# Attention scores of two heads on the two row halves of TensorE, with a fourth bank for max scores and a new order within each pair

## What is computed

```python
q, k, v = split(x @ qkv_w.T + qkv_b)                 # 16 heads of 16
scores  = where(causal, q @ k.T * 16**-0.5, -inf)    # per head 512 x 512
seq_out = softmax(scores) @ v
# memory: lines from x and x_prev, decayed sums over time -> mem_score per head and token
gated   = mean_heads(sigmoid(mem_score * mem_scale) * sigmoid(x @ memg_w.T + memg_b))
x = layernorm(x + (seq_out + gated * (x @ memv_w.T + memv_b)) @ out_w.T + out_b)
x = layernorm(x + sum of 2 of 8 experts, weighted by softmax of the gate logits)
```

## Time and profile before

| | us |
|---|---|
| median of 3 runs | 833.69 (831.81 to 835.61) |
| profiled execution | 833.96, span 832.2 |
| PE / DVE / ACT / POOL busy | 745.5 / 592.8 / 354.1 / 443.3 |
| first exp score of the loop | 77.0 |
| end of the loop, about | 544 |

### The profile page before, as it was taken

The page is one execution under the profiler, slowest core; times in us unless marked ns, Lnnn a source line. Parts: engine busy times, 40 slices in busy tenths (PEclk is TensorE's granted clock), DMA queues, the critical chain, the costliest instruction groups (busy, mean ns, idle before and its releaser), DMA issues.

```text
span 832.2 us, 12627 instructions
## 1 busy us (share of the span) xinstructions
PE 745.5 (90%) x4116; PEld 519.1 (62%) x4116; DVE 592.8 (71%) x2089; ACT 354.1 (43%) x709; POOL 443.3 (53%) x350
## 2 busy tenths in 40 slices
PE   6994998998898999999889998878999999999995
PEld 3552665566465565565555664557788787887884
DVE  2344776778887888888788776635767777677685
ACT  2211555555454455555455465732242342332410
POOL 9200994995676666667475891524254153341510
PEclk9995999999998999999999996979999999999998
DMA  7899599574654655756564556030220302303000
GB/s 272 263 235 175 125 138 144 154 122 97 156 82 96 154 84 112 159 90 146 110 96 112 121 88 214 8 102 0 77 86 18 102 11 91 102 2 102 26 26 26
DMA packets 60421, 89.89 MB, mean 108 GB/s; under 512 B 8234, under 2 KB 37316, under 8 KB 60356
## 3 DMA queue, kind: packets, MB, share of 16 engines
q1 hardware_dynamic: 60356, 89.09, 47.5%
HBM read 54.72 MB, written 33.82 MB: 106 GB/s over the span
## 4 chain that ended last, share of the span: by engine, by line
PE 58%; DVE 18%; DMA 7%; POOL 6%; ACT 5%; issue 4%; SPq 2%; ACTq 0%; POOLq 0%; DVEq 0%
PE ps L1246 21%; PE ps L374 10%; PE ps L338 7%; PE ps L327 7%; PE ps L315 6%; DMA Q<-MT 5%; DVE ps L468 5%; DVE Ob L516 3%; PE ps L232 2%; PE ps L1212 2%; ACT X L1232 1%; DVE Z L1266 1%; ACT Pr L411 1%; PE ps L351 1%; DVE HL L477 1%
## 5 line engine op out<-in xcount | busy, mean ns | idle before, releaser
L468 DVE CUSTOM_DVE_ANT_0 ps<-ps,mask 128x256 f32<-128x256 f32 (+3 forms) x512 | 236.6, 509 | 29.4 <-PE ps L315 28.8
L411 ACT ACTIVATE Pr<-ps 128x512 f32<-128x512 f32 (+2 forms) x384 | 190.1, 527 | 112.3 <-PE ps L327 108.2
L327 PE MATMUL ps<-Q,K 98*128 98x256 f32 (+2 forms) x512 | 172.3, 379 | 27.2 <-DMA Q<-MT 20.0
L1246 PE MATMUL ps<-ew_hi,XT 128*128 128x512 f32 x512 | 181.4, 416 | 0.0
L315 PE MATMUL ps<-K,Q 96*128 96x256 f32 (+2 forms) x512 | 156.9, 352 | 23.2 <-DVE nmax L468 22.8
L1372 DVE SCALAR_TENSOR_TENSOR A<-ps,cw,A 128x256 f32<-128x256 f32 x256 | 123.6, 483 | 54.1 <-PE ps L1246 42.7
L327 PEld LDWEIGHTS ps<-Q,K 98*128 98x128 f32 x512 | 93.7, 196 | 102.0 <-ACT Pr L411 60.4
L612 POOL TENSOR_SCALAR_AFFINE_SELECT Pr<-Pr 128x512 f32<-128x512 f32 x128 | 88.6, 706 | 100.8 <-ACT Pr L411 98.4
L315 PEld LDWEIGHTS ps<-K,Q 96*128 96x128 f32 x512 | 101.6, 201 | 45.0 <-DVE nmax L468 28.6
L1246 PEld LDWEIGHTS ps<-ew_hi,XT 128*128 128x128 f32 x512 | 101.3, 198 | 21.8
L1246 PE MATMUL ps<-ew_rest,XT 128*128 128x512 f32 x256 | 104.8, 409 | 0.0
(11 more groups left out here) (187 smaller groups left out, 1115.8 us busy)
## 6 DMA issues: line engine op xcount, KB each, us to landing
qk_scratch<-HL SPq DMA_DIRECT2D x32, 512.0 KB, 3.2
Q<-qk_scratch SPq DMA_DIRECT2D x96, 128.0 KB, 4.3
K<-qk_scratch SPq DMA_DIRECT2D x96, 128.0 KB, 5.6
Pr<-xT SPq DMA_DIRECT2D x8, 512.0 KB, 6.0
xraw<-xT SPq DMA_DIRECT2D x8, 512.0 KB, 6.4
mem_scratch<-Rl SPq DMA_DIRECT2D x16, 256.0 KB, 6.6
mv_scratch<-MV SPq DMA_DIRECT2D x32, 128.0 KB, 1.7
Wm<-mem_scratch SPq DMA_DIRECT2D x16, 256.0 KB, 9.3
```

The source lines that it names most:

```text
L327: last = nc.tensor.matmul(o, K[0:STACK + 2, hh, P * kt:P * kt + P], Q[0:STACK + 2, hh, T - n:T], start=True, stop=True)
L411: nc.scalar.activation(probs(g % 2, kt, heads[0], len(heads)), src, ACT.Exp, scale=SCALE).then_inc(s_exp, 1)
L468: last = nc.vector.tensor_tensor_reduce(out=scores, in0=scores, in1=mask[:, T - w:T], scale=1.0, scalar=NEG, op0=ALU.add, op1=ALU.max, acc ...
L1246: last = nc.tensor.matmul(o, lhs(c, k), rhs(d, k), start=first, stop=(k == KT - 1 and c == 1))
```

## The change

Q and K hold two heads in the partition range: even heads in rows 0 to 49, odd heads in rows 64 to 113 (48 rows of stack and 2 of maxima; before, each head had columns of its own, in rows 0 to 97). Scores are issued for units u and u+1 together, alternating between the halves, so that neighbouring products use different rows and different banks; units 8 to 11 take heads (0, 2) and (1, 3). Max scores have a fourth bank (ps[5]); the turned outputs use O_ps and the turned maxima J_ps instead of a bank of their own. TensorE's loop goes in steps of two units: exp scores, values, max scores, then at u = 8 the turn of the outputs, at u = 0 and 8 a projection, at u = 4 the turn of the maxima. ScalarE, VectorE take projections at u = 1, 9 and 3, 11; the split of x moves to the end of group 3, two batches ahead. SyncE stores HL's hi and lo one by one, stacks with 8 loads instead of 6 (the same bytes), and stores the maxima with 4 DMAs instead of 2. GpSimd clears K's rows 32 to 63 and 96 to 127 instead of all of Q and K. Not shown below: new sizes of `pick` and `bc` (`BROWS` = 96), a placeholder `later` that keeps the memory places of the last stage, counts of semaphores, and the opening, whose max scores go in calls of 4, 2, 4 and 2 units instead of 3 each.

```diff
@@ -17,7 +17,9 @@
 UNITS = 12
 LEAD = 8
 GROUP = 4
-STACK = 96
+STACK = 48
+HALF = 64
+BROWS = 96
 VW = 17
 NEG = -1e30
 EPS = 1e-5
@@ -71,9 +73,9 @@
 
 
         ps = [ctx.enter_context(nc.psum_tensor(f"ps{i}", [P, BANK], F32)) for i in range(8)]
-        S_ps, ST_ps = ps[0:2] + ps[7:8], ps[2:4]
-        O_ps, OT_ps, J_ps = ps[4:7]
-        M_ps = OT_ps
+        S_ps, ST_ps = [ps[0], ps[1], ps[7], ps[5]], ps[2:4]
+        O_ps, J_ps = ps[4], ps[6]
+        OT_ps, M_ps = O_ps, J_ps
         F_ps, T_ps, L_ps, C_ps = ps[0:4], ps[4:6], ps[6], ps[7]
 
 
@@ -288,7 +291,11 @@
                 return 0, [u]
             if u < 8:
                 return 1, [u - 4]
-            return (2, [2 * (u - 8), 2 * (u - 8) + 1]) if u < 10 else (3, [2 * (u - 10), 2 * (u - 10) + 1])
+            return (2, [u - 8, u - 6]) if u < 10 else (3, [u - 10, u - 8])
+
+        def stacked(t, hh, n):
+
+            return t[HALF * (hh % 2):HALF * (hh % 2) + n, hh // 2, :]
 
         P_OFF = [0, GROUP * 512, GROUP * 896, GROUP * 1152]
 
@@ -303,37 +316,42 @@
 
 
         def pe_max_scores(pe, b, g, u):
-            rank, heads = unit_parts(u)
-            i = QT - 1 - rank
-            n = max(P * (i + 1), 2 * P)
+
             if u == 0:
-                need(pe, s_stack[g], 96, b, 96)
+                need(pe, s_stack[g], 128, b, 128)
             need(pe, s_max, PU, b, UNITS * g + u - 2)
-            for c, h in enumerate(heads):
-                hh = GROUP * g + h
-                o = S_ps[u % 3][:, c * 256:c * 256 + n]
-                last = nc.tensor.matmul(o, Q[0:STACK, hh, P * i:P * i + P], K[0:STACK, hh, 0:n], start=True, stop=True)
-            last.then_inc(s_s, 1)
+            for c in range(len(unit_parts(u)[1])):
+                for v in (u, u + 1):
+                    rank, heads = unit_parts(v)
+                    i, hh = QT - 1 - rank, GROUP * g + heads[c]
+                    n = max(P * (i + 1), 2 * P)
+                    ins = nc.tensor.matmul(S_ps[v % 4][:, c * 256:c * 256 + n], stacked(Q, hh, STACK)[:, P * i:P * i + P],
+                                           stacked(K, hh, STACK)[:, 0:n], start=True, stop=True)
+                    if c == len(heads) - 1:
+                        ins.then_inc(s_s, 1)
 
         def pe_exp_scores(pe, b, g, u):
-            kt, heads = unit_parts(u)
-            n = max(T - P * kt, 2 * P)
+
             if u == 0:
-                need(pe, s_mrow[g], 32, b, 32)
-            need(pe, s_exp, PU, b, UNITS * g + u - 1)
-            for c, h in enumerate(heads):
-                hh = GROUP * g + h
-                o = ST_ps[u % 2][:, c * 256:c * 256 + n]
-                last = nc.tensor.matmul(o, K[0:STACK + 2, hh, P * kt:P * kt + P], Q[0:STACK + 2, hh, T - n:T],
-                                        start=True, stop=True)
-            last.then_inc(s_st, 1)
+                need(pe, s_mrow[g], 64, b, 64)
+            need(pe, s_exp, PU, b, UNITS * g + u)
+            for c in range(len(unit_parts(u)[1])):
+                for v in (u, u + 1):
+                    kt, heads = unit_parts(v)
+                    hh = GROUP * g + heads[c]
+                    n = max(T - P * kt, 2 * P)
+                    ins = nc.tensor.matmul(ST_ps[v % 2][:, c * 256:c * 256 + n],
+                                           stacked(K, hh, STACK + 2)[:, P * kt:P * kt + P],
+                                           stacked(Q, hh, STACK + 2)[:, T - n:T], start=True, stop=True)
+                    if c == len(heads) - 1:
+                        ins.then_inc(s_st, 1)
 
         def pe_values(pe, b, g, kt):
 
             need(pe, s_cm, PU // 3, b, QT * g + kt + 1)
             if kt == 0:
                 need(pe, s_vc, 1, b, 1)
-                need(pe, s_oc, NG, b, g)
+                need(pe, s_on, NG, b, g)
             for h in range(GROUP):
                 last = nc.tensor.matmul(O_ps[32 * h:32 * h + VW, P * kt:T], V[:, kt, GROUP * g + h, :],
                                         probs(g % 2, kt, h, 1)[:, 0, :], start=(kt == 0), stop=(kt == QT - 1))
@@ -342,26 +360,22 @@
 
         def pe_turn_out(pe, b, g):
             need(pe, s_oc, NG, b, g + 1)
-            need(pe, s_on, NG, b, g)
-            ahead_mt = 2 * (g + 3)
-            if isinstance(b, int):
-                ahead_mt = min(ahead_mt, 2 * NG * (NB - b))
-            need(pe, s_mt, 2 * NG, b, ahead_mt)
             for i in range(QT):
                 last = nc.tensor.transpose(OT_ps[:, P * i:P * i + P], Osb[:, P * i:P * i + P], ident[:])
             last.then_inc(s_ot, 1)
 
-        def pe_turn_max(pe, b, g):
+        def pe_turn_max(pe, b, g, projected):
             need(pe, s_max, PU, b, UNITS * (g + 1))
             need(pe, s_mt, 2 * NG, b, 2 * g)
-            need(pe, s_on, NG, b, g - 2)
+            pe.wait_ge(s_lo, projected)
             nc.tensor.transpose(M_ps[0:GROUP * QT, 0:P], nmax[:, g % 2, :], ident[:]).then_inc(s_mtr, 1)
 
-        def pe_project(pe, b, j):
+        def pe_project(pe, b, j, turned=0):
 
             if j == 0:
                 need(pe, s_xlo, 1, b, 1)
             need(pe, s_lo, 8, b, j)
+            need(pe, s_mt, 2, turned, 0)
             first = True
             for k in range(KT):
                 for a, c in ((0, 0), (0, 1), (1, 0)):
@@ -381,23 +395,24 @@
         def pe_batch(pe, b, first=False, last=False):
             for g in range(NG):
                 pb, pg = (b, g - 1) if g else (b - 1, NG - 1)
-                for u in range(UNITS):
+                for u in range(0, UNITS, 2):
                     pe_exp_scores(pe, b, g, u)
+                    if u < 8 and not (first and g == 0):
+                        pe_values(pe, pb, pg, u // 2)
                     on, ng, nu = ahead(g, u)
                     if not (last and on):
                         pe_max_scores(pe, b + on, ng, nu)
-                    if u in (0, 2, 4, 6) and not (first and g == 0):
-                        pe_values(pe, pb, pg, u // 2)
-                    if u in (4, 10) and not last:
-                        pe_project(pe, b + 1, 2 * g + u // 10)
+                    if u == 8 and not (first and g == 0):
+                        pe_turn_out(pe, pb, pg)
+                    if u in (0, 8) and not last:
+                        pe_project(pe, b + 1, 2 * g + u // 8, NG * b + g + 1 + u // 8)
                     if u == UNITS - LEAD and not (last and g == NG - 1):
-                        pe_turn_max(pe, b + (g + 1) // NG, (g + 1) % NG)
-                    if u == 10 and not (first and g == 0):
-                        pe_turn_out(pe, pb, pg)
+                        pe_turn_max(pe, b + (g + 1) // NG, (g + 1) % NG, min(8 * (b + 1) + 2 * g + 1, 8 * NB))
                     if last and (g, u) == (2, 8):
                         pe_gates(pe)
                     if last:
                         last_phase["tensor"]["beside"](pe, g, u)
+                        last_phase["tensor"]["beside"](pe, g, u + 1)
 
 
         def act_exp(act, b, g, u):
@@ -442,10 +457,10 @@
                 pb, pg = (b, g - 1) if g else (b - 1, NG - 1)
                 for u in range(UNITS):
                     act_exp(act, b, g, u)
-                    if g == 0 and u == 0 and not last:
-                        act_split_x(act, b + 1)
-                    if u in (4, 10) and not last:
-                        act_project(act, b + 1, 2 * g + u // 10)
+                    if u in (1, 9) and not last:
+                        act_project(act, b + 1, 2 * g + u // 9)
+                    if (g, u) == (NG - 1, 10) and b < NB - 2:
+                        act_split_x(act, b + 2)
                     if u == 7 and not (first and g == 0):
                         act_out(act, pb, pg)
                     if g == 0 and u == 8:
@@ -464,10 +483,10 @@
             need(dve, s_s, PU, b, UNITS * g + u + 1)
             w = P * (i + 1)
             for c, h in enumerate(heads):
-                scores = S_ps[u % 3][:, c * 256:c * 256 + w]
+                scores = S_ps[u % 4][:, c * 256:c * 256 + w]
                 last = nc.vector.tensor_tensor_reduce(
                     out=scores, in0=scores, in1=mask[:, T - w:T], scale=1.0,
-                    scalar=NEG, op0=ALU.add, op1=ALU.max, accum_out=nmax[:, g % 2, QT * h + i:QT * h + i + 1])
+                    scalar=NEG, op0=ALU.add, op1=ALU.max, accum_out=nmax[:, g % 2, turned_row(h, i):turned_row(h, i) + 1])
             last.then_inc(s_max, 1)
 
         def dve_project(dve, b, j):
@@ -523,14 +542,14 @@
                     on, ng, nu = ahead(g, u)
                     if not (last and on):
                         dve_max(dve, b + on, ng, nu)
-                    if g == 0 and u == 0 and not last:
-                        dve_split_x(dve, b + 1)
-                    if u in (5, 11) and not last:
+                    if u in (3, 11) and not last:
                         dve_project(dve, b + 1, 2 * g + u // 11)
-                    if u == UNITS - LEAD and not (last and g == NG - 1):
```

(53 more changed lines are left out.)

47 lines of the change are left out of this document (28 added, 19 removed).

## The result

The changed kernel takes 883.25 us (median of 4 runs, 878.97 to 887.22), the kernel before 834.65 on the same chip: a ratio of 1.0589 (95% interval 1.0529 to 1.0649). I had forecast 815 and at most 838. The forecast is wrong in sign: slower by 49 us.

A forecast was written before the change was run, and what follows sets the result against it. The loop was taken as bound by TensorE's order in quiet groups, elsewhere by VectorE or the row store's detour behind HL. Savings by stretch of 2, 1, 15, 0 and 1, together 19 us from 833.96, gave 815, range 806 to 825.

The forecast's parts named there:

- Halves side by side: Score products of a pair on two row halves overlap in TensorE: a gain of 2.6 us per group, bounds 0 and 2.6.
- changes between kinds of product: Projections and turns interrupt half-array work on TensorE three times per group, in and out: 0.3 us each, 0.9 in all.
- The end of a quiet group: A row store of maxima, not TensorE, sets a quiet group: next group starts at 12.5 to 13.6, so 13.1 us.
- Exp scores in lock step with ScalarE: An exp pair waits until ScalarE has read both banks of the pair before: TensorE waits 1.4 us per group.
- The signs that were named for a wrong forecast: Loop groups not falling to about 14.3 us, paired products starting 0.1 or more apart, or clock below 0.9 from 0.95.
- HL stores: In group 1, exps and TensorE wait 1.1 us for both stores, landing taken as 3.2; 0.2 us per group on the mean.
- the opening: Before the loop's start at 77.0 us, halved stores and two more row issues: 0, bounds -1 and +1.2 us.
- VectorE and the scans: VectorE's waits (71.2 us in all) mostly go, but scans ahead of MT lengthen some loop groups: mean 14.1 us per group.
- The number of DMAs: Four row stores per group instead of two: three issues before the last at 0.6 us each on a quiet group's path.
- The slower rival: The four row stores decide: landings of 5 us make each of 24 groups 15.7 instead of 15.0; 851 us, chance 0.16.
- The detour behind the HL store: The row store of maxima queues behind the HL store in SyncE: 1.9 us, gone in two of four groups.
- The clock: Granted clock of the loop, 0.95; falling below 0.9 as TensorE's idle time grows was a sign of a wrong forecast.

The follow-up runs named there:

- the repaired kernel: Changed kernel with outer count 16 in the HL store, max scores ahead of values, and each pair of row stores joined into one: 827.65 us, ratio 0.9954.

## Why the prediction was wrong

**Halves side by side**: right at the full clock. 13.0 less 2.6 and with 0.9 for changes between kinds of product makes 11.3 of work for TensorE in a quiet group; this is the one of 523 to 535.5:
```profile
523.00:535.50 12.50, 11.43 (x83) 6.03 (x83) 9.26 (x42) 6.92 (x15) 12.35 (x6) 1.00 0.27 85
```
The saving itself was a little less than it reads: of the 13.0 before TensorE was busy 12.7, so 1.3 us went, not 1.7. **The end of a quiet group**: right, 12.5 on the row store, where 12.5 to 13.6 stood. **Exp scores in lock step with ScalarE**: right in kind, 44.9 us of waits where before
```profile
PE ps L327 <- ACT Pr L411: 6.8, 20, 0.8
```
In the quiet group of 523 they are only 0.2 us, though, where the sum had 1.4. The signs that were named for a wrong forecast both came: groups of 16.9 where 14.3 were needed, and a clock below 0.9.

**"HL stores" and "the opening": the first step that failed.** I took the landing of 3.2 us from the row of the old store and kept it for the new one, with 0.2 us per group and nothing in the opening. I halved the bytes and did not look at the shape. The destination's outermost count goes from 128 to 8, the landing to 4.7 to 5.3, and two stores must land before HL is free. Measured: +7.3 in the opening; 36 us as the only edit; 18.5 back when only that count is changed, and with it 20 of the +31 in groups 1. The rule stands in the Trainium skill, in the section cited above; the forecast didn't apply it to the stores.

**"VectorE and the scans": the second.** I let VectorE's waits "mostly go" since the turns were no longer behind a projection, and had VectorE start at 5.2 in the path to MT without asking what it did before and between. The max scores of a pair moved behind eight value products and its supply became bursts of four units; the fourth bank can't help, since the units are not there. 100 us of waits for TensorE became 142. Max scores first gives back 19 and 28 us in the two kernels where it is clear of noise.

**The number of DMAs: the third.** Row stores were priced on one path of a quiet group, and the extra load issues (eight for six per group) not at all. In the kernel before, twelve loads and four row stores cost 16 us. The slower rival had the row stores and a size (851), but as a landing behind the bulk store; the chain of a slow group shows the HL store and ScalarE instead.

**The detour behind the HL store**: priced at 1.9 us in half of the groups, some 30 us; taking it away alone gives at most 5. Something else of the group comes next at once, which the chain of one moment does not show.

**The clock: at nothing in the sum.** It stood among the signs and had no price. At 0.80 in the long stretch TensorE is busy 252.8/18 = 14.0 us per group, in a quiet group at 1.00 11.4: the sum had 11.3 for it everywhere. How much of these 2.6 us reaches the kernel's time is open.

The parts alone (36, 25 and 16 us, less the 18 that halves bring in the repaired kernel) come to 59, the change to 49: they cover one another in part. It is a rough sum, since the 16 are with 12 loads and since halves in the old order brought nothing but a loss. Open: what the lower clock costs by itself, why halves in the old order lose 24 us more than their DMAs alone (the clock of 0.83 there is an untested candidate), and the shares of loads and row stores.

## What to carry to other kernels

When an edit changes a DMA's layout, price it anew by its outermost counts on both sides, not by its bytes; a store on which a buffer waits is as much on the path as a product. When the order within a block is rewritten, write down for each consumer the gaps between its supplies, since a wait that is removed is of use only if none as long opens elsewhere. Take away a suspected wait alone before counting on it: here that experiment would have shown that the detour was worth next to nothing.

## What the runs showed of the hardware

- The second of two stores of 256 KB, issued 0.8 us after the first, lands after 4.7 to 5.3 us with 8 outermost in the destination of both and after 2.9 with 16; one store of 512 KB with 128 rows took 2.6.
- One VectorE operation with two inputs in SBUF took two to three times its time beside a GpSimd operation, in two of its eight runs. The split of x in the changed kernel:
```profile
274.76 2.90 POOL L876 TENSOR_TENSOR Ob<-Ob,Rl 128x1533 f32<-128x1533 f32 x1 [1.66 <-DVE Ob L535]
275.39 3.36 DVE L529 TENSOR_TENSOR xlo<-xraw,xhi 128x1024 fp32r<-128x1024 f32 x1
...
278.80 1.22 PE L388 MATMUL ps<-xhi,wqk 128*128 128x512 f32 x2 [3.71 <-DVE xlo L529]
```
Its median is 1.22. GpSimd is done at 277.66, and the split 1.09 later, as if it began only then. The next GpSimd operation, L878 at 277.75, takes 4.31 us instead of its usual 3.45, so it loses time too. The Trainium skill (SBUF — State Buffer, Who interferes with whom) calls this an exclusive lock on shared ports, and the rows agree. It was there before the change too (2.63 at 254.85), but the projection that now waits for it stands in front of other work for 3.71 us.
- More TensorE work raised the granted clock over the kernel (0.896 to 0.934) and still cost 21 us.
- The same four 256-column score products take 0.80 us at the lower level (274.30) and 0.50 at the higher (524.45); a pair of 512 columns 0.79 and 0.49.
